# A state-space scan kernel: each state's drive made in two halves, each with its own correction and signal

## The reference, cut to what matters

```python
def step(h, inp):
    dt_t, B_t, C_t, x_t = inp
    dA = jnp.exp(dt_t[..., None] * A)
    h = dA * h + dt_t[..., None] * B_t[:, None, :] * x_t[..., None]
    y = jnp.sum(h * C_t[:, None, :], axis=-1)
    return (h, y)
_, ys = lax.scan(step, h0, xs)
y = ys.transpose(1, 0, 2) + D * xc
y = y * _silu(z)
```

## Time and profile before

| | before |
|---|---|
| median of 3 runs | 1763.05 us |
| the profiled execution | 1760.51 us |
| its span | 1757.8 us |
| VectorE busy | 1559.0 us (89%) |
| TensorE matmul busy | 1537.0 us (87%) |
| ScalarE busy | 1437.1 us (82%) |
| GpSimd busy | 1251.3 us (71%) |
| drive multiplies, L796 | 256 of 2358 ns, 603.6 us |
| drive corrections, L803 | 256, 55.0 us |
| scans, L960 | 512 of 1221 ns, 616.4 us |

### The profile page before, as it was taken

One profiled execution on the slowest core, in us unless ns is written; L12 is line 12 of the kernel. 1 busy time (PEld: TensorE's weight loads), 2 busy tenths in 40 slices (PEclk: granted clock), 3 DMA queues, 4 the chain that ended last, 5 costly groups with the idle time before them and its releaser, 6 DMA issues.

```text
span 1757.8 us, 26243 instructions
## 1 busy us (share of the span) xinstructions
PE 1537.0 (87%) x7512; PEld 1153.3 (66%) x7512; DVE 1559.0 (89%) x2887; ACT 1437.1 (82%) x3076; POOL 1251.3 (71%) x1314
## 2 busy tenths in 40 slices
PE   3766888989898998989898998989898998999875
PEld 2354767767676776667676776767676776777653
DVE  4889999999999999999999999999999999999711
ACT  2466888888998988898998988898998988898632
POOL 2557668787787769687787768687777869686422
PEclk8577999999999999999999999999999999999987
DMA  8111111111111111111111111111111111111100
GB/s 206 51 35 51 46 58 48 49 55 55 43 49 56 54 50 55 49 54 54 44 49 55 52 53 55 50 55 49 42 57 52 47 61 55 43 56 48 31 0 12
DMA packets 68452, 91.58 MB, mean 52 GB/s; under 512 B 15742, under 2 KB 34758, under 8 KB 68310
## 3 DMA queue, kind: packets, MB, share of 16 engines
q1 hardware_dynamic: 64566, 89.73, 17.0%
q10 hardware_dynamic: 3744, 0.18, 0.1%
HBM read 85.17 MB, written 4.72 MB: 51 GB/s over the span
## 4 chain that ended last, share of the span: by engine, by line
POOL 27%; PE 25%; DVE 17%; ACT 16%; issue 13%; DMA 1%; POOLq 0%; ACTq 0%; SPq 0%; DVEq 0%
POOL drive L796 10%; PE bank L339 10%; PE bank L455 6%; DVE unit L960 4%; POOL wide L845 3%; DVE hc L967 2%; ACT unit L571 2%; PE y_ps L365 2%; POOL wide L850 2%; POOL wide L847 2%; ACT hx L550 1%; ACT ops L537 1%; DVE xc L992 1%; ACT L537 1%; PE bank L326 1%
## 5 line engine op out<-in xcount | busy, mean ns | idle before, releaser
L796 POOL TENSOR_TENSOR drive<-wx,rows 128x1024 f32<-128x1024 f32 x256 | 603.6, 2358 | 154.8 <-DMA rows<-rows_scratch 78.5
L960 DVE TENSOR_TENSOR_SCAN unit<-unit,drive 128x512 f32<-128x512 f32 x512 | 616.4, 1221 | 36.5 <-POOL drive L803 27.7
L571 ACT ACTIVATE unit<-dt,aneg 128x254 f32<-128x254 f32 x1024 | 441.8, 468 | 8.0
L967 DVE TENSOR_TENSOR hc<-unit,rows 128x512 f32<-128x512 f32 x512 | 340.5, 683 | 5.6
L365 PE MATMUL y_ps<-ident,hc 128*128 128x128 f32 x2048 | 275.3, 280 | 65.8 <-DVE hc L967 65.7
L365 PEld LDWEIGHTS y_ps<-ident,hc 128*128 128x128 f32 x2048 | 239.1, 144 | 120.0 <-DVE hc L967 79.2
L339 PE MATMUL bank<-w_l,ops 128*128 128x256 f32 x768 | 194.0, 397 | 15.0 <-DVE xc L995 8.9
L339 PEld LDWEIGHTS bank<-w_l,ops 128*128 128x128 f32 x768 | 144.8, 195 | 65.5 <-DVE xc L995 20.5
L571 ACT ACT_TABLE_LOAD x109 | 139.8, 1283 | 1.9
L580 ACT ACTIVATE carry<-unit 128x4 f32<-128x4 f32 x512 | 79.1, 169 | 67.5 <-DVE unit L974 62.8
L455 PE MATMUL bank<-ops,w_f 128*128 128x256 f32 x512 | 116.2, 386 | 10.9 <-ACT ops L537 10.9
(11 more groups left out here) (229 smaller groups left out, 3150.0 us busy)
## 6 DMA issues: line engine op xcount, KB each, us to landing
rows<-rows_scratch SPq DMA_DIRECT2D x256, 256.0 KB, 3.4
x_t<-in_L_attn_x_dram SPq DMA_DIRECT2D x16, 256.0 KB, 3.8
xs<-in_L_attn_x_dram SPq DMA_DIRECT2D x16, 256.0 KB, 3.5
out_dram<-xs SPq DMA_DIRECT2D x16, 256.0 KB, 2.2
w_f<-in_L_attn_ffn_w_dram SPq DMA_DIRECT2D x2, 1024.0 KB
ops<-in_L_ffn_qweights_dram SPq DMA_DIRECT2D x1, 1536.0 KB, 15.2
w_in<-in_L_attn_in_proj_w_dram SPq DMA_DIRECT2D x1, 1024.0 KB, 5.2
hq_t<-attn_in_proj_weight_dram SPq DMA_DIRECT2D x1, 768.0 KB
```

The lines of the kernel that those rows point to most:

```text
L571: last = a_.activation(u[:, k * TOK:(k + 1) * TOK].rearrange("p (b t) -> p b t", b=B)[:, :, 1:TC], dt[p][:, g, :].rearrange("p (b t) -> p ...
L796: g_.tensor_tensor(drive[n % 2][:, :, :].rearrange("p (g b) t -> p g b t", b=B), wx[p][:, :, :].rearrange("p g (b t) -> p g b t", b=B), ro ...
L960: v.tensor_tensor_scan(u[:, :], u[:, :], d, 0.0, ALU.mult, ALU.add).then_inc(S["scan_done"], 1)
L967: v.tensor_tensor(hc[n % NPROD][:, 4 * half:4 * half + 4, :].rearrange("p (g b) t -> p g b t", b=B), unit_of(ch, n, half)[:, :].rearrange( ...
```

## The change

Each state's drive is made by two multiplies of two channel groups each, 128x512, and each is followed by its own correction of four columns and its own signals, so that `drive_ready` counts four instead of two for a state. Half 0 waits for the scans up to n-2's a half (2n-3), and half 1 for those up to n-2's b half (2n-2). Each scan half now waits for its own half of the drive. The wait for the carried state (`carry_in`, states 0 and 8) stands before the first multiply instead of before the correction.

```diff
-    carry_in=2, decay_ready=2 * NS, drive_ready=2 * NS, scan_done=2 * NS, hc_done=2 * NS, carry_saved=2 * NS,
+    carry_in=2, decay_ready=2 * NS, drive_ready=4 * NS, scan_done=2 * NS, hc_done=2 * NS, carry_saved=2 * NS,
...
-                pool.wait_ge(*at("scan_done", ch, 2 * n - 2))
-                g_.tensor_tensor(drive[n % 2][:, :, :].rearrange("p (g b) t -> p g b t", b=B),
-                                 wx[p][:, :, :].rearrange("p g (b t) -> p g b t", b=B),
-                                 rows[n % NROWB][:, 0, :].rearrange("p (b t) -> p b t", b=B)[:, None, :, :]
-                                 .to_broadcast([P, DG, B, TC]), ALU.mult).then_inc(S["drive_ready"], 1)
-                pool.wait_ge(*at("drive_ready", ch, 2 * n + 1))
                 if n % 8 == 0:
                     pool.wait_ge(*at("carry_in", ch, 1 + n // 8))
-                g_.tensor_tensor(drive[n % 2][:, :, 0], drive[n % 2][:, :, 0], fix[:, n, :], ALU.add)\
-                    .then_inc(S["drive_ready"], 1)
+                for half in range(2):
+                    g, s = slice(2 * half, 2 * half + 2), slice(4 * half, 4 * half + 4)
+                    pool.wait_ge(*at("scan_done", ch, 2 * n - 3 + half))
+                    g_.tensor_tensor(drive[n % 2][:, s, :].rearrange("p (g b) t -> p g b t", b=B),
+                                     wx[p][:, g, :].rearrange("p g (b t) -> p g b t", b=B),
+                                     rows[n % NROWB][:, 0, :].rearrange("p (b t) -> p b t", b=B)[:, None, :, :]
+                                     .to_broadcast([P, 2, B, TC]), ALU.mult).then_inc(S["drive_ready"], 1)
+                    pool.wait_ge(*at("drive_ready", ch, 4 * n + 2 * half + 1))
+                    g_.tensor_tensor(drive[n % 2][:, s, 0], drive[n % 2][:, s, 0], fix[:, n, s], ALU.add)\
+                        .then_inc(S["drive_ready"], 1)
...
-                if half == 0:
-                    dve.wait_ge(*at("drive_ready", ch, 2 * n + 2))
+                dve.wait_ge(*at("drive_ready", ch, 4 * n + 2 * half + 2))
```

## The result

The changed kernel takes 1808.4 us (median of 4 runs, 1807.4 to 1810.7) beside 1763.0 us for the kernel before (4 runs, 1762.3 to 1764.0): a ratio of 1.0259, 95% interval 1.0241 to 1.0277. It is 45 us slower. The profiled execution took 1807.35 us, with a span of 1805.6 us; the one of before took 1760.51. The forecast was 1808.

The account below looks back on a forecast made before the run. VectorE is busiest, but the path runs through GpSimd's drives and op's norm, closing each period. Op's norm +1.64, rounding +0.95 and x1 +0.50 give +3.1 us, times 15 = +46: 1808 us, range 1772 to 1832.

Parts of the forecast that it names:

- (a) The cost of a split drive: GpSimd's drives: half a multiply 1.27 us, the pair 3.00, 0.41 more per drive, 105 us more GpSimd time over 256.
- (b) The four drives in front of op's norm: GpSimd's gapless stretch, drive1 to drive4: 4 x 0.41 = +1.64 us a period on the path.
- (c) The waits that go: VectorE's waits before scan14a (0.52 us) and scan1a (up to 1.29): -0.52 at the rounding, scan1a's gain worth nothing.
- (d) The rounding: VectorE's L939 to L946 and drive0's halves exclude each other before xout: +0.95 us a period, in place of -0.52.
- x1: VectorE's L1042 beside GpSimd's j1in, made later by drive7 and drive8: +0.5 us a period, bounds 0 and 0.82.
- The covers: drive5, drive6 and drive9 to drive13: additions hidden by GpSimd's existing waits, costing nothing; 0.41 us each without cover.
- The sum: Whole period: +1.64 + 0.95 + 0.50 = +3.1 us, times 15 = +46 us, forecast 1808.
- The lower end of the range: Kernel time without collisions at the lower bound for op's norm's four drives: 1763 + 15 x 0.6 = 1772.
- VectorE binds: Rival: VectorE's in-order stream sets the period, so the removed 1.81 us comes back: -27 us, 1736; chance 0.07.
- No collisions: Rival: VectorE's operations pass the halves or take gaps between them: +1.12 us a period, +17 us, 1778; chance 0.24.
- nothing: Rival: op's norm has slack but scans stay pinned by their exponentials, path unchanged: 1763; chance 0.06.
- more collisions: Rival: one more turn a period lost behind a half multiply: 4.4 us a period, 1827; chance 0.13.

Follow-up runs that it names:

- whole_signal: Changed kernel, but both scans of a state wait for the whole drive, still made in halves; 1808.6 us.
- carry_back: Changed kernel with the wait for fix0 put back behind the first multiply, ahead of its correction; 1802.6 us.
- s1to4: Changed kernel with only the drives of states 1 to 4 in halves, the other twelve whole; 1794.9 us beside 1761.0.
- split_seven: Changed kernel with only the drives of states 5, 6 and 9 to 13 in halves; 1765.4 us beside 1760.6.
- eleven-drive kernel: Changed kernel with op's norm ahead of drive4 and states 0, 7, 8, 14 and 15 whole again, the other eleven in halves; 1785.9 us.

## Why the prediction was right, and where it was not

*(a) The cost of a split drive* was right: half a multiply 1.27 us, the pair 3.01 from start to start, +0.42 against the +0.41 of the working. The mean of a multiply is that of L787, which it had been taken from. GpSimd's busy time grew by 83 us, not 105: the 105 counted the gaps between instructions, and the busy column does not. (Its 78% of the span would have been 77, and was 74.)

*(b) The four drives in front of op's norm:* +1.64 predicted, +1.61 to +1.63 measured, and shown to be these four by splitting only them.

*(c) The waits that go* did go, and brought nothing, as the prediction said of scan1a; whole_signal shows it for all of them. For scan1a the reason that it gave was incomplete. It called VectorE's gain "off the path", as if VectorE had room. It has none: the drive's wait was replaced by one for the exponential (0.79 us at 904.57, where 1.29 stood before), and VectorE's stream as a whole is level with the path through op's norm, by 0.1 us in before and 0.5 in after. VectorE's idle time before scans went only from 36.5 to 29.2 us, with the exponentials as the new releaser.

*(d) The rounding:* +0.95 predicted, +1.2 to +1.26 measured. The picture was the right one, with drive0's second half between the first and second step of the rounding: L941 came 0.47 us earlier and was stopped by the first half (1.16 us), L944 took 1.53 us behind the second, and xout followed. The part that was mis-sized is the moved wait for fix0, which the prediction put "under 0.1 us in a place already counted": it stood for 0.27 us, shown twice (carry_back -0.27, s1to4 +0.28). Without it the term is 0.98. The Trainium skill, "SBUF — State Buffer", section "Who interferes with whom", states that a VectorE operation with two SBUF inputs, or one in a two-port mode, and a GpSimd one exclude each other for the whole instruction. That is borne out at each of these places, by 1.53 us where 0.43 is normal, for one. A detail was named wrongly: L783 was not the operation caught under L1000, but L779 (1.72 us for 0.70) and arg (1.64 for 0.60) were.

*x1:* +0.5 predicted, +0.35 measured. j1in did start 0.34 us later after op's norm (26.00 against 25.65), but L1043 did not; it started when it had (26.9) and was stopped for 0.3 us longer. That is the term at its size, within its bounds of 0 and 0.82, in the changed kernel. In every kernel here L1043 ends 0.54 us after j1in's end, once that is later than its own 0.69 us would make it (all 148 stopped ones of the thirteen traces, within 0.03 us): with j1in starting 25.78, 25.90 and 26.00 us after op's norm it takes 0.82, 0.93 and 1.00. But drives 7 and 8 are not the only thing that makes j1in late: with both whole and 5 and 6 split it starts at 25.90, since VectorE, stopped beside drive5's second half (L226 of that kernel, 0.58 us for 0.24), is later with the scan for which drive8 waits.

*The covers* held for GpSimd, and were thought of for GpSimd alone. The working priced drives 5 and 6 at nothing; split with 9 to 13, and without 7 and 8, they go with +0.25 us a period at x1 (split_seven; drives 9 to 13 lie behind it in GpSimd's list). drive5 has cover behind it, but its halves lie beside VectorE's L220 and L224. There a single multiply is one instruction to wait for and two halves are two, with a VectorE operation caught by each. In the changed kernel op's norm is later and hides most of them: from it to L1043's start are 26.9 us, as before, but the 0.17 us that L1039 waited for TensorE in before is gone. In the eleven-drive kernel, with the norm early, they had nothing to hide behind. The 3.7 us of busy time that VectorE gained each period are such stops. Its groups by form in the changed kernel:

```profile
L944 DVE TENSOR_SCALAR q<-q 128x512 f32<-128x512 f32 x16 | 22.2, 1390 | 0.6
...
L220 DVE TENSOR_SCALAR j_scl<-j_amax 128x44 f32<-128x44 f32 x32 | 20.2, 632 | 1.1
...
L224 DVE TENSOR_SCALAR j_rcp<-j_rcp 128x44 f32<-128x44 f32 x32 | 17.9, 561 | 1.1
...
L941 DVE TENSOR_SCALAR q<-q 128x512 int32<-128x512 int32 x16 | 17.5, 1092 | 0.4 <-POOL q L864 0.4
L1043 DVE TENSOR_TENSOR xs<-xs,s 128x512 f32<-128x512 f32 x16 | 15.6, 976 | 0.5
...
L1064 DVE TENSOR_SCALAR sd<-sd 128x32 f32<-128x32 f32 x16 | 9.7, 603 | 0.6
```

and three of them in before:

```profile
L220 DVE TENSOR_SCALAR j_scl<-j_amax 128x44 f32<-128x44 f32 x32 | 10.1, 315 | 1.1
L942 DVE TENSOR_SCALAR q<-q 128x512 f32<-128x512 f32 x16 | 6.8, 427 | 0.5
L224 DVE TENSOR_SCALAR j_rcp<-j_rcp 128x44 f32<-128x44 f32 x32 | 6.0, 187 | 1.1
```

These three have 15.4 + 10.1 + 11.9 = 37.4 us more in the span, and VectorE as a whole 52 (1611.3 against 1559.0), with instructions that did not change.

*The sum* was +3.1 a period and is +3.14, and the times say 45.4 us more against its 46. A part of that closeness is luck: one term was 0.3 too small, another 0.15 too large, and "paid once a period, some 15 times" isn't how it came about. The first two periods paid nothing in front of op's norm (-0.5 and +0.2 us), and some 3 of the 44.7 us of the fourteen whole periods are two more periods with a lowered clock. The lower end of the range rests on a slip: its own 0.92 - 0.52 is 0.4 a period and not 0.6, so 1769 and not 1772, which changes nothing here. And the sum was made on one path. For an edit that shortens that path, as moving op's norm, the same way of reckoning gave 1772 and was wrong by 34 us, because a second path lay 0.5 us below. *VectorE binds*, the rival at 0.07, was the half of the truth that the working lacked: VectorE's stream does bind next, only it was lengthened by the change and not shortened. *No collisions* (1778) is excluded by the time, and *nothing* (1763) too, as is *more collisions* (1827), though further stops did come, at L220 and L224.

Still open: why the clock fell in more periods of some kernels than of others, and so how far the medians of kernels with few drives split can be compared. No kernel here was clearly faster than before.

## What to carry to other kernels

A split on one engine costs its fixed parts at every place and pays only where the consumer's wait stands on the path; price it place by place, since here seven of the drives cost 5 us, and two others 16, each with some 4 us for the moved wait in it. When the two engines stop one another, every further piece also gives the other engine one more chance to be stopped, so look at what it runs beside the pieces, even where the splitting engine has room. And before a removed wait or a reordered step is counted as a gain, ask how far behind the next path lies: an engine that is busy 93.8 of 98.5 us has a path of its own, whatever the chain of waits names.

## What the runs showed of the hardware

**Very small VectorE operations are stopped too.** L224 on 128x44 normally takes 0.19 us and took 1.00 beside the second half of drive5 (921.94 to 923.21, with L224 from 922.26 to 923.26), and L1064 on 128x32 took 603 ns in the mean instead of 181. L222, the reciprocal between L220 and L224, kept its 0.43 us in the same period.

**How late a stopped operation ends.** At the places shown here it is its own length less some 0.15 us after the end that the trace shows for GpSimd's: L944 0.29 us (0.43 by itself), L1043 0.54 (0.69), L224 0.05 (0.19). So the price of a stop can be read off the two start times and GpSimd's length.

**A stopped instruction counts as busy.** Of a busy share that rises with unchanged instructions, here from 1559 to 1611 us, the rise is waiting.

**The clock.** In 5 of 14 periods of the changed kernel the last stage, from x1's norm to log, took 29.3 us instead of 27.7. The windows of the same four microseconds of that stage, in an undisturbed period and in a disturbed one, are not the same in TensorE's granted clock:

```profile
454.40:458.40 4.00, 4.00 (x25) 3.14 (x23) 3.85 (x6) 3.95 (x9) 3.84 (x6) 1.00 0.05 17
```

```profile
556.00:560.00 4.00, 4.00 (x12) 2.61 (x11) 2.27 (x4) 2.75 (x8) 3.84 (x6) 0.59 0.06 19
```

and in the timeline the same eight matmuls take 1.89 and 3.50 us, at 2.4 and mostly 1.2 GHz:

```profile
454.05 1.89 PE L339 MATMUL bank<-w_qkv,ops 128*128 128x256 f32 x8
...
555.73 3.50 PE L339 MATMUL bank<-w_qkv,ops 128*128 128x256 f32 x8
```

Just ahead of them TensorE had been idle for 1.07 and 1.08 us, waiting for ScalarE (L628), and had then run four matmuls on 16 rows (L409) and four by `ident` (L431) in both periods; the clock fell in one and not in the other. Such periods were 3 of 14 in before, 10 with drives 1 to 4 split, 8 without them, and 1 in the kernel with seven drives split. At 1.6 us each they move a kernel's time by up to 10 us, and the edits meant to touch nothing in that stage; what decides it isn't shown. It is why the terms of a change are to be read from undisturbed periods and not from the medians alone.
